# Reordering TensorE's slots in the self attention of a kernel's last stage, with scores three pieces ahead

## What is computed

```python
def _attention(src, Wq, bq, Wk, bk, Wv, bv, Wo, bo):
    B, T, d = src.shape
    scale = HEAD_DIM ** (-0.5)
    q = (src @ Wq + bq).reshape(B, T, NHEAD, HEAD_DIM)
    k = (src @ Wk + bk).reshape(B, T, NHEAD, HEAD_DIM)
    v = (src @ Wv + bv).reshape(B, T, NHEAD, HEAD_DIM)
    scores = jnp.einsum('bqhd,bkhd->bhqk', q, k) * scale
    probs = jax.nn.softmax(scores, axis=-1)
    out = jnp.einsum('bhqk,bkhd->bqhd', probs, v).reshape(B, T, d)
    return out @ Wo + bo
...
attn_out = _attention(src, Wq, bq, Wk, bk, Wv, bv, Wo, bo)
x = _ln(src + attn_out, ln1_g, ln1_b)
ff = _moe(x, gW, gb, W1, b1, W2, b2)
return _ln(x + ff, ln2_g, ln2_b)
```

## Time and profile before

| | us |
|---|---|
| median of 3 runs (2423.55 to 2425.49) | 2424.04 |
| the profiled execution | 2430.15 |
| its span, first to last instruction | 2428.3 |
| of which the self attention of stage C | some 305 |

### The profile page before, as it was taken

One profiled execution on the slowest core, in us unless ns is written; L12 is line 12 of the kernel. 1 busy time (PEld: TensorE's weight loads), 2 busy tenths in 40 slices (PEclk: granted clock), 3 DMA queues, 4 the chain that ended last, 5 costly groups with the idle time before them and its releaser, 6 DMA issues. The chain is left out here.

```text
span 2428.3 us, 45160 instructions
## 1 busy us (share of the span) xinstructions
PE 2046.4 (84%) x17914; PEld 1362.0 (56%) x17914; DVE 1585.8 (65%) x3854; ACT 1320.4 (54%) x2169; POOL 534.5 (22%) x476
## 2 busy tenths in 40 slices
PE   4779997466499999999999999999996888878997
PEld 3546665243255655555565565556564565556776
DVE  4834453677478778788788778778862566653443
ACT  3645553465326666666666666656673545543333
POOL 1410001443122122122122122212212233211111
PEclk8789997565569999999999999999997889969999
DMA  5036662000122232233233223223212100000000
GB/s 158 1 92 179 195 180 65 4 14 21 51 94 94 80 115 104 73 110 114 67 108 115 76 102 113 82 93 114 101 56 93 35 29 24 1 1 4 8 8 11
DMA packets 89103, 181.18 MB, mean 75 GB/s; under 512 B 5906, under 2 KB 63162, under 8 KB 88510
## 3 DMA queue, kind: packets, MB, share of 16 engines
q1 hardware_dynamic: 88894, 178.30, 22.4%
HBM read 95.24 MB, written 11.65 MB: 44 GB/s over the span
## 5 line engine op out<-in xcount | busy, mean ns | idle before, releaser
L1407 DVE TENSOR_REDUCE b_part_max<-psum 128x1 f32<-128x482 f32 (+3 forms) x1248 | 737.4, 650 | 188.3 <-PE psum L1284 174.2
L1197 ACT ACTIVATE b_PT<-psum 128x800 f32<-128x800 f32 x768 | 616.3, 836 | 386.3 <-PE psum L1303 380.1
L1284 PE MATMUL psum<-b_KH,b_QBD 64*128 64x482 f32 (+1 forms) x1152 | 422.5, 445 | 45.8 <-DVE b_part_max L1407 43.4
L1303 PE MATMUL psum<-b_QS,b_KS 64*128 64x200 f32 x3072 | 438.4, 288 | 0.5 <-ACT b_PT L1197 0.3
L1303 PEld LDWEIGHTS psum<-b_QS,b_KS 64*128 64x128 f32 x3072 | 339.4, 186 | 16.2 <-issue 11.8
L1319 PE MATMUL psum<-b_PT,b_V 128*32 128x200 f32 x6144 | 341.3, 339 | 0.6 <-ACT b_PT L1197 0.6
L1284 PEld LDWEIGHTS psum<-b_KH,b_QBD 64*128 64x128 f32 x1152 | 197.4, 189 | 198.1 <-DVE b_part_max L1407 118.3
L1120 POOL TENSOR_TENSOR b_KL<-b_KF,b_KH 128x1444 fp32r<-128x1444 f32 x32 | 106.9, 3341 | 693.0 <-PE psum L1303 670.0
L1319 PEld LDWEIGHTS psum<-b_PT,b_V 128*32 128x32 f32 x6144 | 160.0, 109 | 149.2 <-ACT b_PT L1197 82.3
L2095 DVE SCALAR_TENSOR_TENSOR c_U<-psum,c_gt,c_U 100x128 f32<-100x128 f32 x256 | 72.1, 344 | 130.3 <-PE psum L1916 130.0
L384 POOL TENSOR_TENSOR a_rs<-a_ve,a_half 100x4 f32<-100x4 f32 x48 | 49.1, 1022 | 426.2 <-DVE a_ve L757 426.2
(11 more groups left out here) (274 smaller groups left out, 3235.0 us busy)
## 6 DMA issues: line engine op xcount, KB each, us to landing
b_KS<-b_KH SPq DMA_DIRECT2D x64, 722.0 KB
a_CT<-in_ctxt SPq DMA_DIRECT2D x32, 722.0 KB, 4.2
b_CT<-in_ctxt SPq DMA_DIRECT2D x32, 722.0 KB, 4.3
b_KS<-b_KL SPq DMA_DIRECT2D x32, 722.0 KB
a_CN<-in_ctxn SPq DMA_DIRECT2D x32, 704.0 KB
att_scratch<-b_AO SPq DMA_DIRECT2D x32, 200.0 KB, 1.9
c_AIN<-att_scratch SPq DMA_DIRECT2D x8, 800.0 KB
b_MB<-in_mask SPq DMA_DIRECT2D x32, 180.5 KB, 4.4
```

Of the source, the lines that this page charges most:

```text
L1197: nc.scalar.activation(PT[:, kt % 2, 2 * a:2 * a + 2, :], psum[:, 2 * a:2 * a + 2, 0:TG], ACT.Exp).then_inc(sem["pt_ready"], 1)
L1284: m = mm(bank(b, D, size), QBD[rows, j % 2, tile * D:(tile + 1) * D], KH[rows, j % 2, at_:at_ + size], start=True, stop=True)
L1303: m = mm(bank(p, D, 2 * T, (s % 2) * 2 * T), KS[rows, j % 2, s, kt * D:(kt + 1) * D], QS[rows, j % 2, s * 2 * T:(s + 1) * 2 * T], start=Tr ...
L1407: v.tensor_reduce(part_max[0:rows, q, c:c + 1], bank(b, rows, CHUNKS[c][1]), AX.X, ALU.max)\
```

## The change

TensorE's slot gets another order: turn_pieces(k), back (even slots), the projections, scores(k+3), weigh(k); in slot 5 of a unit weigh(k) comes ahead of scores(k+3). Scores are thus one piece further ahead, and so are subtract and exponent: VectorE runs subtract(k+2) and ScalarE exponent(k+2) in slot k, and one more of each ahead of the loop. P has three buffers in place of two; the score banks stay two pairs. Two waits for divide are added, in turn0 and for one unit in turn2, where they were implied before. No arithmetic is changed, and no DMA.

```diff
--- before.py
+++ after.py
@@ -1468,7 +1468,7 @@
         FK = sb("FK", [D, 2, TG])
         KBD = sb("KBD", [D, 2, GROUP, TG])
         VS = sb("VS", [T, 2, GROUP, HEADS, 32])
-        P = sb("P", [T, 2, HQ // 2])
+        P = sb("P", [T, 3, HQ // 2])
         PT = sb("PT", [T, 2, 2, TG])
         OS = sb("OS", [D, TG])
         U = sb("U", [T, 2, GROUP, D])
@@ -1636,7 +1636,7 @@
 
             def exponent(k):
                 act.wait_ge(sem["sub_ready"], k + 1)
-                nc.scalar.activation(P[:, k % 2, :], P[:, k % 2, :], ACT.Exp).then_inc(sem["fe_ready"], 1)
+                nc.scalar.activation(P[:, k % 3, :], P[:, k % 3, :], ACT.Exp).then_inc(sem["fe_ready"], 1)
 
             def keep(k):
                 act.wait_ge(sem["fpT_psum"], k + 1)
@@ -1692,6 +1692,7 @@
             queries(0)
             values(0)
             exponent(0)
+            exponent(1)
             for k in range(PIECES):
                 b, s = divmod(k, SLOTS)
                 if s % 2 == 0 and k:
@@ -1701,8 +1702,8 @@
                 if s == 5 and b:
                     middle(b - 1)
                 keep(k)
-                if k + 1 < PIECES:
-                    exponent(k + 1)
+                if k + 2 < PIECES:
+                    exponent(k + 2)
                 if s == 1 and b:
                     turned1(b - 1)
                 if s == 1 and b >= 2:
@@ -1767,6 +1768,8 @@
 
             def turn0(u):
                 pe.wait_ge(normed[0], u + 1)
+                if u:
+                    pe.wait_ge(sem["fu_ready"], (u - 1) * GROUP + 1)
                 if u >= 2:
                     pe.wait_ge(sem["r_used"], u - 1)
                 turn(H[:, u % 3], turned[0])
@@ -1806,7 +1809,7 @@
                 if k:
                     pe.wait_ge(sem["fpT_ready"], k)
                 for a in range(8):
-                    x_ = nc.tensor.transpose(bank(4 + a // 4, T, T, (a % 4) * T), P[:, k % 2, t.ts_(a)], ident[0:T, 0:T])
+                    x_ = nc.tensor.transpose(bank(4 + a // 4, T, T, (a % 4) * T), P[:, k % 3, t.ts_(a)], ident[0:T, 0:T])
                 x_.then_inc(sem["fpT_psum"], 1)
 
             def weigh(k):
@@ -1867,6 +1870,7 @@
                     pe.wait_ge(sem["fv_ready"], u + 3)
                 elif u < LAST:
                     pe.wait_ge(sem["r_used"], u + 1)
+                    pe.wait_ge(sem["fu_ready"], BATCH - 1)
                 else:
                     pe.wait_ge(sem["u_ready"], 2)
                 turn(Y[:, u], turned[2])
@@ -1924,13 +1928,12 @@
             values(0)
             scores(0)
             scores(1)
+            scores(2)
             for k in range(PIECES):
                 b, s = divmod(k, SLOTS)
-                if k + 2 < PIECES:
-                    scores(k + 2)
+                turn_pieces(k)
                 if s % 2 == 0 and k:
                     back(k // 2 - 1)
-                turn_pieces(k)
                 if s == 0 and b >= 2:
                     gate(b - 2)
                 if b < LAST:
@@ -1951,7 +1954,12 @@
                         outer(b - 1)
                     if s == 7:
                         turn2(b - 1)
-                weigh(k)
+                if s == 5:
+                    weigh(k)
+                if k + 3 < PIECES:
+                    scores(k + 3)
+                if s != 5:
+                    weigh(k)
             pe.wait_ge(sem["big_loaded"], 32)
             back(BATCH - 1)
             gate(LAST - 1)
@@ -2015,10 +2023,10 @@
                 dve.wait_ge(sem["fs_psum"], k + 1)
                 sc = psum[0:T, 2 * p:2 * p + 2, 0:TG].rearrange("p b (h k) -> p b h k", h=4)
                 link(v.tensor_reduce(peak[:, p, :], sc, AX.X, ALU.max))
-                if k >= 2:
-                    dve.wait_ge(sem["fpT_psum"], k - 1)
+                if k >= 3:
+                    dve.wait_ge(sem["fpT_psum"], k - 2)
                 for b in range(2):
-                    last = v.tensor_tensor(P[:, p, b * TG:(b + 1) * TG].rearrange("p (h k) -> p h k", h=4), sc[:, b, :, :],
+                    last = v.tensor_tensor(P[:, k % 3, b * TG:(b + 1) * TG].rearrange("p (h k) -> p h k", h=4), sc[:, b, :, :],
                                            peak[:, p, 4 * b:4 * b + 4].unsqueeze(2).to_broadcast([T, 4, T]), ALU.subtract)
                 last.then_inc(sem["sub_ready"], 1)
 
@@ -2101,6 +2109,7 @@
             enter(0)
             shift(0, 0)
             subtract(0)
+            subtract(1)
             for k in range(PIECES):
                 b, s = divmod(k, SLOTS)
                 if s % 2 == 0 and k:
@@ -2109,8 +2118,8 @@
                     gate_first(b - 2)
                 if s == 5 and b:
                     shift(1, b - 1)
-                if k + 1 < PIECES:
-                    subtract(k + 1)
+                if k + 2 < PIECES:
+                    subtract(k + 2)
                 if b >= 2:
                     if s == 4:
                         gate_top(b - 2)
```

## The result

The changed kernel takes 2517.75 us in the median of 6 runs (2505.03 to 2527.53), the kernel before 2424.36 (2421.56 to 2436.91). The ratio is 1.037, with a 95% interval of 1.034 to 1.040: 93 us slower. The prediction had 2442, and slower as the likeliest; the time lies 61 us above the upper end of its range.

A forecast was written before the change was run, and what follows sets the result against it. TensorE's own order sets the pace, so its idle time decides. Units 1 to 6 +19.2, unit 0 -1.5, unit 7 -3, clock +3 make +17.7 us: median 2442 us, range 2419 to 2457 (the forecast's own 2434 to 2450).

The forecast's parts named there:

- Direction: Whole kernel: slower by over 0.2% (4.8 us), chance 0.70; faster 0.16, within it 0.14.
- The four returns of bank 7: Slots 0, 2, 4, 6: nothing stands between back and the projection, 0.93 us of idle TensorE each.
- the wait in slot 5: Slots 4 and 5: scores' wait, bound by keep, exponent and queries' copy on ScalarE, stays; the stretch grows 0.8 us.
- The sum without the clock: Self attention: 3.2 us a unit, 19.2 us for units 1 to 6; unit 0 -1.5 us, unit 7 -3 us.
- Unit 0: First unit, without gate, outer or turn1: -1.5 us, bounds -3.5 and +1.
- Unit 7: Last unit, without next unit's projections, where looking ahead works best: -3 us, bounds 0 and -10.
- The clock: Self attention: more idle time makes low-clock stretches likelier; +3 us, bounds -11 (none left) and +11 (twice as many).
- TensorE works in time in which it would have waited: Clock term: the reason low stretches, though likelier, were priced at only +3 us.
- Rival 4: Self attention: the clock falls more, +30 us, 2454 us; chance 0.20.
- Rivals 1 to 3: Waits just go: 2403, chance 0.10; clock pays: 2419 or half way 2426, 0.13; no look-ahead at all: 2424, 0.07.
- Rival 1: Look-ahead frees weigh and scores, other cover is found for back's return: 2424 - 21 = 2403 us; chance 0.10.
- The step on slots 0 and 1: Enter, behind the later subtract(3), holds up turn1; TensorE idles 1.8 us, the stretch from back grows 1.5 us.

The follow-up runs named there:

- the run with filled gaps: Changed kernel plus 61 filling matmuls: behind back in even slots, two each ahead of turn1 and turn0, one behind queries; 2430.07 us, ratio 1.002.
- the order-only kernel: Changed kernel's slot order on TensorE, but scores only two pieces ahead and two probability buffers, as before the change; 2483.22 us, ratio 1.024.

## Why the prediction was wrong

- **Direction, place, new waits: right.** The four returns of bank 7 lie open (0.77 us idle each where I had 0.93), turn1 waits 1.63 us for enter (1.8), weigh's wait for keep is left in one place of units 1 to 5, scores' wait for subtract in none, turn0 still waits for residual (0.5 us). What lies ahead of the loop and behind it keeps its time within 1 us. One reading was off without effect: the row of the wait in slot 5 names GpSimd's spreading of the keys as what released scores, not ScalarE.
- **The sum without the clock: right, as far as the run with filled gaps can show it.** A unit at the high clock was to take 39 us; there it took 39.44 and 39.46 at 1.00. Unit 0, taken at -1.5 us, is 1.8 shorter (35.63 against 37.45). Unit 7, from back to back, takes 30.10 us (2151.25 to 2181.35) in place of 38.64 (2141.49 to 2180.13): 8.5 less, between the 3 taken and the bound of 10. The loop is 4.8 us longer; the prediction's terms with no low clock left give 19.2 - 1.5 - 3 - 11 = 3.7. That the two are so near is partly luck: a unit costs more than was said (3.7 us over unit 1 before, in place of 3.2 us) and unit 7 gains more.
- **The clock: this step failed.** I took +3 us with a bound of +11, "twice as many" of the low stretches that the kernel before shows. It is about +82, counted like that term from the kernel before (the 93 us of the loop less the 11 that were lost already). The credits for the loop's ends went with it: in the changed kernel unit 0 took 44.54 us in place of 37.45, and unit 7, from back to back, 38.47 in place of 38.64. I had scaled what the trace before shows: there, in units 2 to 6, the low clock comes in stretches of some 4 to 8 us between which the engine finds back. In the changed loop it mostly does not. At the low clock the same pair of slots keeps TensorE busier, and yet each pair still has its gap of 0.77 us; units 1 and 2 ran at 0.56 and TensorE was busy 48.68 of 54.30 us. Unit 7 before, at a mean of 0.60 over 38 us and at the low clock for its last 20, was the row that showed such a standing low state. The prediction priced only what it could gain. What keeps the clock low in the changed loop stays open: the open return goes with it, but a kernel with the same waits ran at 0.70 to 0.74, and work added elsewhere raised the clock with the return open.
- **"TensorE works in time in which it would have waited": wrong in size.** I held that a low clock is mostly hidden in a loop with more idle time. But TensorE's work of about 30 us a unit at the high clock is near 50 at the low one (29.22 us in unit 1 before at 1.00, 48.68 after at 0.56), above everything that the waits could hide.
- **Rival 4 named the mechanism** (the clock falls more) and priced it at 2454 by the same bound. Rivals 1 to 3 fell. Rival 1 counted the look-ahead at up to 21 us of gain; in the old order, and a whole piece further ahead on TensorE, it cost 11 us.
- The step on slots 0 and 1 was right in its wait, but taking the wait away gave 4 us at most and not 10. The wait went over to back (11.7 us in 10 places, 1.3 in 2 without it), behind the later subtract.

## What to carry to other kernels

Before an instruction is moved, ask what wait it covers now, above all a return trip through another engine on a shared PSUM bank; moved ahead of the trip's start it covers nothing. Write out the sequence of the engine before and after: it shows by how much an instruction really comes earlier, which the number in its name (k+2 or k+3) doesn't. In a loop whose main engine is near its limit, price a new idle place not by its own length (here 0.8 us, some 20 us in sum) but also by what TensorE's clock does: look for a stretch of the trace in which the clock stays low, and compute the whole loop at that level as the outer bound. A filling matmul in the gap is a cheap test of whether the clock or the wait costs the time; put in another place as well, it tells whether the gap matters or only the added work.

## What the runs showed of the hardware

- TensorE's clock can stay at its low level with the engine some 90% busy and no single wait over 1.63 us: 45 us at 0.50 with 41.01 us of busy time. Before the change, unit 1 held 1.00 with TensorE busy 29.22 of 35.71 us and waits up to 1.10 us.
- 30 matmuls more, in gaps of under 1 us, made the kernel 66 us faster; the same 30 beside the gaps, which stayed open, 23 us.
- Transpositions in those gaps keep the clock up as ordinary matmuls do (2454.77 and 2451.26 us).
- The changed kernel's times spread over 22 us (2505.03 to 2527.53), those of the run with filled gaps over 5 us (2429.05 to 2434.12). A lower clock alone doesn't bring the spread: the order-only kernel at 0.70 to 0.74 has 5 us, too (2482.41 to 2487.72).
